# One VectorE addition of p for all four rows, and fixed places for the FFN's VectorE operations

## What is computed

```python
def _derivative(q, p, drive, coupling, bias):
    i_couple = jnp.tanh(q) @ coupling.T
    dq = q - q ** 3 / 3.0 - p + drive + i_couple + bias
    dp = EPSILON * (q + ALPHA - BETA * p)
    return (dq, dp)
# per token: dq1..dq4 at q, q + DT/2 dq1, q + DT/2 dq2, q + DT dq3
q_next = clip(q + DT / 6.0 * (dq1 + 2 * dq2 + 2 * dq3 + dq4), -20, 20)
p_next = clip(p + DT / 6.0 * (dp1 + 2 * dp2 + 2 * dp3 + dp4), -20, 20)
...
h = silu(gate) * up
y = h @ w_down.T
out = x + y / sqrt(mean(y * y) + EPS)
```

## Time and profile before

| | us |
|---|---|
| median of three executions | 1601.17 |
| profiled execution | 1600.72 |
| its span in the trace | 1598.8 |
| VectorE busy | 1521.6 (95%) |
| TensorE busy | 1468.2 (92%) |
| ScalarE busy | 784.6 (49%) |
| GpSimd busy | 48.3 (3%) |

### The profile page before, as it was taken

One profiled execution on the slowest core, in us unless ns is written; L12 is line 12 of the kernel. 1 busy time (PEld: TensorE's weight loads), 2 busy tenths in 40 slices (PEclk: granted clock), 3 DMA queues, 4 the chain that ended last, 5 costly groups with the idle time before them and its releaser, 6 DMA issues.

```text
span 1598.8 us, 97361 instructions
## 1 busy us (share of the span) xinstructions
PE 1468.2 (92%) x39808; PEld 1323.3 (83%) x39808; DVE 1521.6 (95%) x11790; ACT 784.6 (49%) x5087; POOL 48.3 (3%) x49
## 2 busy tenths in 40 slices
PE   0057899999999999999999999999999999999997
PEld 0046788898988898898988989888888989898897
DVE  7989999999999999999999999999999999999992
ACT  4134455555555555545555555555455555555552
POOL 3410000000000000000000000000000000000000
PEclk9999999999999999999999999999999999999999
DMA  9400000000000000000000000000000000000000
GB/s 238 120 6 7 13 7 8 17 8 20 8 7 21 7 21 4 21 7 8 20 8 21 8 17 8 17 11 7 20 8 20 5 20 8 8 21 7 21 4 22
DMA packets 13554, 33.13 MB, mean 21 GB/s; under 512 B 1712, under 2 KB 6064, under 8 KB 12976
## 3 DMA queue, kind: packets, MB, share of 16 engines
q1 hardware_dynamic: 13104, 26.89, 6.4%
HBM read 22.69 MB, written 4.19 MB: 17 GB/s over the span
## 4 chain that ended last, share of the span: by engine, by line
PE 82%; DVE 11%; issue 1%; ACT 0%; POOL 0%; POOLq 0%; DVEq 0%; ACTq 0%
PE scan_ps L584 54%; PE gu_ps L322 19%; PE y_ps L336 9%; DVE q_stage L702 1%; DVE th L663 1%; DVE q_sq L667 1%; DVE q_stage L704 1%; DVE with_q L657 1%; DVE with_p L657 1%; DVE xl L374 1%; DVE scan_ps L675 1%; DVE q_cub L670 1%; DVE p_part L657 1%; DVE q_raw L704 0%; DVE h L353 0%
## 5 line engine op out<-in xcount | busy, mean ns | idle before, releaser
L584 PE MATMUL scan_ps<-th,wscan 128*128 128x32 f16 (+1 forms) x32768 | 1080.3, 175 | 121.6 <-ACT th L620 115.1
L584 PEld LDWEIGHTS scan_ps<-th,wscan 128*128 128x128 f16 x32768 | 956.5, 96 | 255.6 <-ACT th L620 177.1
L620 ACT ACTIVATE th<-q_stage 128x16 f16<-128x16 f32 x1536 | 318.8, 208 | 512.9 <-DVE q_stage L702 512.9
L322 PE MATMUL gu_ps<-xl,wffn 128*128 128x128 f16 x2816 | 384.9, 219 | 0.0
L322 PE MATMUL gu_ps<-xh,wffn 128*128 128x128 f16 x2816 | 384.5, 218 | 0.0
L663 DVE TENSOR_TENSOR th<-t,th 128x16 f16<-128x16 f32 x2048 | 343.6, 168 | 0.0
L622 ACT ACTIVATE t<-q_stage 128x16 f32<-128x16 f32 x1536 | 306.4, 199 | 0.0
L322 PEld LDWEIGHTS gu_ps<-xl,wffn 128*128 128x128 f16 x2816 | 272.8, 97 | 0.3
L322 PEld LDWEIGHTS gu_ps<-xh,wffn 128*128 128x128 f16 x2816 | 262.8, 97 | 0.3
L620 ACT ACTIVATE th<-q_raw 128x16 f16<-128x16 f32 x512 | 106.3, 208 | 206.8 <-DVE q_raw L702 203.3
L428 ACT ACTIVATE sum_r<-dr,constant 128x64 f32<-128x64 f32 x528 | 174.0, 332 | 7.6 <-DMA dr<-drive 7.6
(11 more groups left out here) (43 smaller groups left out, 1018.2 us busy)
## 6 DMA issues: line engine op xcount, KB each, us to landing
raw<-packed SPq DMA_DIRECT2D x11, 768.0 KB, 6.4
dr<-drive SPq DMA_DIRECT2D x34, 128.0 KB, 2.1
sc<-scales SPq DMA_DIRECT2D x11, 384.0 KB, 6.8
xres<-x SPq DMA_DIRECT2D x16, 256.0 KB, 3.5
out<-osb SPq DMA_DIRECT2D x16, 256.0 KB, 2.9
coup<-coupling_t SPq DMA_DIRECT2D x1, 1024.0 KB, 15.0
q_raw<-cond_t SPq DMA_DIRECT2D x1, 16.0 KB, 1.8
bias<-bias_t SPq DMA_DIRECT2D x1, 2.0 KB, 1.7
```

The lines of the kernel that those rows point to most:

```text
L322: i = nc.tensor.matmul(gu_ps[b][:, half * P:(half + 1) * P], wffn[:, u, part, col:col + P], tokens[f.parity][:, kt, :], start=(r == 0), st ...
L584: i = nc.tensor.matmul(to if both else to[:, 0], wscan[:, w, part, kt, cols], moving if both else moving[:, 0], start=first, stop=last, sk ...
L620: nc.scalar.activation(th[s % 2][:, c, 0, :], q[:, c, :], ACT.Tanh, scale=1.0 / S).then_inc(now.tanh_hi, 1)
```

## The change

`UNIT` scales rows 1 to 3 so that p enters every row with the same factor. One addition of 128 columns then forms `with_p` for all four rows, in kind 3, with `p_state` read four times by a broadcast. The row's own unit is multiplied in where the row joins the cube (`local_in` in place of `cube_in`), and the factor of the cube moves into `square`. In kinds 1 and 2 the additions for row 3 and for p that stood between `square` and `low_part` stand behind `local_in`; some move one stage on; the one for q3 moves from the end of kind 2 to the head of kind 3. `Places` gives each h32, hl and norm_out a stage of its own of kind 1 or 2, `hist_low` has stages 1 and 2 with two each, `hh` shares h32's stage, and `DOWN_LAG` is 7.

```diff
-P_ROW = [float(LINEAR[i, BY_P] * P_UNIT) for i in range(ROWS)]
+P_ALL = float(np.float32(LINEAR[0, BY_P] * P_UNIT))
+def row_unit(i):
+    at = np.float32(LINEAR[i, BY_P] * P_UNIT / P_ALL).view(np.int32)
+    near = [float((at + np.int32(k)).view(np.float32)) for k in range(-4, 5)]
+    qs = LINEAR[i, BY_Q1:BY_Q1 + i]
+    return min(near, key=lambda unit: abs(sum(float(np.float32(x / unit)) * unit - x for x in qs)))
+UNIT = [1.0] + [row_unit(i) for i in range(1, ROWS)]
+BY = LINEAR[:-1] / np.array(UNIT)[:, None]
-SHIFT = [(COEF[STAGE_COEF[i]] + LINEAR[i, BY_Q1 + i]) / CUBE[i] for i in range(4)]
+OWN = [COEF[STAGE_COEF[i]] + float(LINEAR[i, BY_Q1 + i]) for i in range(4)]
-LOCALS = STEPS * 23
+LOCALS = STEPS * 20
-DOWN_LAG = 5
+DOWN_LAG = 7
-def off_start(s):
-    return s if s % 4 else s + 1
+class Places:
+    def __init__(self):
+        self.taken = {1, 2}
+    def next(self, s):
+        while s % 4 not in (1, 2) or s % STAGES in self.taken:
+            s += 1
+        self.taken.add(s % STAGES)
+        return s
 class Schedule:
...
+        places = Places()
         self.silu = {s + 1: u for u, s in gate_up.items()}
-        self.h32 = {off_start(s + 2): u for u, s in gate_up.items()}
-        self.hh = {s + 3: u for u, s in gate_up.items()}
-        self.hl = {off_start(s + 4): u for u, s in gate_up.items()}
+        self.h32, self.hh, self.hl = {}, {}, {}
+        for u, s in gate_up.items():
+            at = places.next(s + 2)
+            self.h32[at] = self.hh[at] = u
+            self.hl[places.next(at + 1)] = u
...
-        busy = set(self.h32) | set(self.hl) | {s + STAGES for s in (*self.h32, *self.hl)}
-        free = [s for s in range(self.norm_sum + 3, 2 * STAGES) if s not in busy and s % 4]
-        self.norm_out = {s: n for n, s in enumerate(free[:KT])}
+        self.norm_out = {}
+        for n in range(KT):
+            self.norm_out[places.next(max([self.norm_sum + 3, *self.norm_out]))] = n
...
-        with_p = [sb(f"with_p{i}", [P, KT, B]) for i in range(ROWS)]
+        with_p = sb("with_p", [P, ROWS, KT, B])
...
-                if ffn and s == 0:
-                    act.wait_ge(before.clipped, STEPS)
-                    hist_high(act, now, 0)
-                if ffn and s == 1:
-                    hist_high(act, now, 1)
-                    hist_high(act, now, 2)
-                if ffn and s == 2:
-                    hist_high(act, now, 3)
+                if ffn and s in (0, 1):
+                    if s == 0:
+                        act.wait_ge(before.clipped, STEPS)
+                    for c in range(s * HC, (s + 1) * HC):
+                        hist_high(act, now, c)
...
-            def square(q):
-                return local(nc.vector.tensor_tensor(q_sq[:, :, :], q, q, ALU.mult))
+            def square(i, q):
+                return local(nc.vector.scalar_tensor_tensor(q_sq[:, :, :], q, CUBE[i], q, ALU.mult, ALU.mult))
...
-            def cube_in(s):
+            def local_in(s):
                 i = s % 4
-                nc.vector.scalar_tensor_tensor(local_ps, halves(q_cub[:, :, :]), CUBE[i],
-                                               halves(linear[i][:, :, :]), ALU.mult, ALU.add).then_inc(now.first_half, 1)
-
-            def add_p(row, step):
-                return add(with_p[row][:, :, :], p_state[:, :, :], P_ROW[row], sum_r[:, step % STEPS, row])
+                nc.vector.scalar_tensor_tensor(local_ps, halves(linear[i]), UNIT[i], halves(q_cub[:, :, :]),
+                                               ALU.mult, ALU.add).then_inc(now.first_half, 1)
+
+            def add_p(step):
+                p_rows = p_state[:, :, :].unsqueeze(1).to_broadcast([P, ROWS, KT, B])
+                return add(with_p[:, :], p_rows, P_ALL, sum_r[:, step % STEPS])
+
+            def add_q(to, row, column, q, base):
+                return add(to[:, :, :], q, float(BY[row, column]), base)
...
-                if ffn and s == 1:
-                    hist_low(dve, now, 0)
-                if ffn and s == 2:
-                    hist_low(dve, now, 1)
-                    hist_low(dve, now, 2)
-                if ffn and s == 3:
-                    hist_low(dve, now, 3)
+                if ffn and s in (1, 2):
+                    for c in range((s - 1) * HC, s * HC):
+                        hist_low(dve, now, c)
...
-                if t == HS:
-                    dve.wait_ge(now.sum_r_ready, SUM_R_PARTS)
-                add_p(2, t)
+                if ffn and t == 1:
+                    dve.wait_ge(now.xl_ready, KT)
...
-                ffn_part(s)
-                add_p(3, t)
                 low_part(s, 0)
...
                 s = 4 * t + 1
                 ffn_part(s)
                 dve.wait_ge(now.q_ready, 2 * s)
-                squared = square(q2)
-                add(with_q1[2][:, :, :], q1, float(LINEAR[3, BY_Q1]), with_p[3][:, :, :])
+                squared = square(1, q2)
                 low_part(s, 0)
...
-                cube_in(s)
+                local_in(s)
+                add_q(with_q1[2], 3, BY_Q1, q1, with_p[:, 3])
                 add(p_part[0][:, :, :], p_state[:, :, :], P_SUM[0], q1)
-                add(with_q2[0][:, :, :], q2, float(LINEAR[2, BY_Q2]), with_q1[1][:, :, :])
-                add(with_q2[1][:, :, :], q2, float(LINEAR[3, BY_Q2]), with_q1[2][:, :, :])
+                add_q(with_q2[0], 2, BY_Q2, q2, with_q1[1][:, :, :])
                 finish(s)
 
                 s = 4 * t + 2
                 ffn_part(s)
                 dve.wait_ge(now.q_ready, 2 * s)
-                squared = square(q3)
-                add(p_part[1][:, :, :], p_part[0][:, :, :], P_SUM[1], q2)
+                squared = square(2, q3)
                 low_part(s, 0)
...
-                cube_in(s)
+                local_in(s)
+                p2 = add(p_part[1][:, :, :], p_part[0][:, :, :], P_SUM[1], q2)
+                with_23 = add_q(with_q2[1], 3, BY_Q2, q2, with_q1[2][:, :, :])
+                dve.wait_ge(now.local, p2)
                 add(p_part[2][:, :, :], p_part[1][:, :, :], P_SUM[2], q3)
-                add(with_q3[:, :, :], q3, float(LINEAR[3, BY_Q3]), with_q2[1][:, :, :])
                 finish(s)
 
                 s = 4 * t + 3
-                ffn_part(s)
+                dve.wait_ge(now.local, with_23)
+                add_q(with_q3, 3, BY_Q3, q3, with_q2[1][:, :, :])
                 dve.wait_ge(now.q_ready, 2 * s)
...
                 if t + 1 == HS:
-                    dve.wait_ge(now.sum_r_ready, 2 * KT)
+                    dve.wait_ge(now.sum_r_ready, SUM_R_PARTS)
                 if t + 1 == STEPS:
-                    dve.wait_ge(now.sum_r_ready, SUM_R_PARTS + 2 * KT)
+                    dve.wait_ge(now.sum_r_ready, 2 * SUM_R_PARTS)
                 dve.wait_ge(now.local, p_next)
-                add_p(0, t + 1)
-                add_p(1, t + 1)
+                add_p(t + 1)
                 finish(s)
```

More of the change, by code:

```diff
@@ L429, in sum_drive @@
                                  bias=constant[:, row, c:c + 1],
-                                 scale=float(LINEAR[row, BY_R] * S)).then_inc(done, 1)
+                                 scale=float(BY[row, BY_R] * S)).then_inc(done, 1)
         def sp_store(sp, f, k):
@@ L508, in _ @@
                 for row in range(ROWS):
-                    nc.vector.tensor_scalar(constant[:, row], bias[:, :], float(LINEAR[row, BY_R] * S),
-                                            float(LINEAR[row, BY_ONE] * S), ALU.mult, ALU.add).then_inc(constants, 1)
+                    nc.vector.tensor_scalar(constant[:, row], bias[:, :], float(BY[row, BY_R] * S),
+                                            float(BY[row, BY_ONE] * S), ALU.mult, ALU.add).then_inc(constants, 1)
                 dve.wait_ge(constants, ROWS)
@@ L537, in _ @@
                 dve.wait_ge(sums_set, SUM_R_PARTS)
-                for row in (0, 1):
-                    nc.vector.scalar_tensor_tensor(with_p[row][:, :, :], p_state[:, :, :], P_ROW[row],
-                                                   sum_r[:, 0, row], ALU.mult, ALU.add)
+                p_rows = p_state[:, :, :].unsqueeze(1).to_broadcast([P, ROWS, KT, B])
+                nc.vector.scalar_tensor_tensor(with_p[:, :], p_rows, P_ALL, sum_r[:, 0], ALU.mult, ALU.add)
                 for n, coef in enumerate(COEF):
@@ L644, in dve_block @@
         def dve_block(dve, now, before, ffn, rest):
-            linear = [with_p[0], with_q1[0], with_q2[0], with_q3]
+            linear = [with_p[:, 0], with_q1[0][:, :, :], with_q2[0][:, :, :], with_q3[:, :, :]]
             count = [0]
@@ L714, in dve_block @@
                     dve.wait_ge(before.local, LOCALS)
-                if t == HS:
-                    dve.wait_ge(now.sum_r_ready, SUM_R_PARTS)
-                add_p(2, t)
+                if ffn and t == 1:
+                    dve.wait_ge(now.xl_ready, KT)
                 if t:
-                    if ffn and t == 1:
-                        dve.wait_ge(now.xl_ready, KT)
```

(19 more changed lines are left out.)

3 lines of the change are left out of this document (2 added, 1 removed).

## The result

The changed kernel takes 1562.89 us (median of four executions, 1562.32 to 1563.14) against 1601.2; the ratio is 0.9761, 95% interval 0.9746 to 0.9775. A second series gave 1563.41 us and 0.9762 (0.9749 to 0.9775). The forecast was 1553 with a range of 1536 to 1580: the direction and the range held, but 48 us were forecast and 38 came.

What follows compares the result with a forecast made beforehand. It took the first low part (next reduce 0.73 us later), then VectorE's queue, as the bound. Fifteen blocks save 44.6 us, the first block 2.8, the tail 0.8: 48.2 in all, giving 1553 us, range 1536 to 1580.

Steps and rivals of the forecast that it cites:

- The limit: In each stage the next reduce follows the first low part by 0.73 us; VectorE's queue is a second limit.
- Wide addition: End of kind 3: one 128-column addition costs 0.20 us, the same as the two 32-column ones there.
- Kind 2 with hl: Stages with hl: second reduce 0.17 behind the first, local term at R+0.93, stage 1.38 us.
- The wait for p's sum: In kind 2 the third addition waits for the first: 0.22 us behind it instead of 0.10.
- One sign that the prediction had named for a free wait: Kind 2 no longer than kind 1 would show that VectorE's wait for its own result costs nothing.
- Kind 3: Loses its FFN operation; p's addition stays ahead of the low part at R+0.62: stage 1.35 us.
- The burst stage: One kind 3 stage per block, with the last unit's down matmuls, keeps about 0.77 us extra.
- First block: Earlier low part saves 0.06 us in kinds 1 and 2, 0.04 in kind 0, 0.02 in kind 3: 2.8 us.
- A: Low part does not bind in clean stages; only the FFN stages' 0.07 us goes: 1558 to 1582 us; 30%.
- B: VectorE binds less; all stages fall to 1.33 to 1.345 us, total 1525 to 1536 us; 12%.
- C: The wide addition's broadcast operand is slow in kind 3: 1596 us at 0.41, 1614 at 0.48; 8%.
- D: A down matmul finding hl late stops TensorE's in-order queue, 50 us at 0.3 each: 1603 us; 3%.

Runs made afterwards that it cites:

- W and P without O: The changed kernel with row 3's addition (kind 1) and p's addition (kind 2) back between square and first low part: 1598.01 us, ratio 0.9977.
- W: The kernel before with only the wide addition, rows and FFN operations as before: 1597.51 us, ratio 0.9975.
- the last kernel: The changed kernel with two hist_low as one 256-column operation, the xl wait left out and the cleared-semaphores wait moved: 1558.39 us, ratio 0.9736.

## Why the prediction was right, and where it fell short

- **Where the 10.7 us went.** The profiled execution was to gain 48.2 us and gained 37.5. Of the difference 10.5 us lie in the fifteen blocks. Their mean by kind is 22.10, 22.06, 22.66 and 22.59 us against 21.9, 22.0, 22.4 and 22.4. The first block, the tail and the preparation make up the rest.
- **The limit.** Right: a low part, not TensorE's filling work, sets a stage (W and P without O, fewer matmuls). Wrong in which one: the prediction read 0.73 behind the first low part. The second one binds, 0.53 to 0.54 behind it, and since it mostly lay 0.19 behind the first, the two readings gave the same numbers; that the law held in the sum is in part luck. Where the cube waits for a late square between them, the second one is later than that, and 0.73 is too little.
- **Wide addition.** Right in its price: the reduce stands 0.25 behind it, as it did behind the two narrow ones. Four narrow ones at that place would have given back all but 1 us of the gain.
- **Kind 0** 1.37, kind 1 1.36 and 1.34: as forecast. A pair of hist_low in kind 1 too (1.54 for 1.56).
- **Kind 2 with hl**, the mis-sized term: 1.38 forecast, 1.405 measured. The sum hides two errors that partly cancel. The local term came at R+0.97, not 0.93; behind it stand 0.43 to the next reduce, where the prediction's chain has 0.12 + 0.22 + 0.12 = 0.46 (from 0.93 that gives 1.39, not the 1.38 that it wrote). The step that failed is "the second reduce comes 0.17 behind the first". That holds behind kind 0, where the distance is 0.17. Behind kind 1 it is 0.19 to 0.20, and hl, the square and all that follows stand 0.03 later. Why it is longer there is argued and not tested: kind 1 ends at 1.35 with the low parts' limit at 1.33 to 1.35, so its first reduce is hardly late, and the second has to wait for TensorE's second half. Together 11 stages, two norm_out and the pair, 14 x 0.025 x 15 = 5 us. Empty kind 2 stages, two per block, took 1.34 for 1.37, since there the local term was in time and the chain behind it shorter.
- **The wait for p's sum** in kind 2: 0.22 from addition to addition, as forecast, and of that 0.02 is lost, since another addition fills the rest. Against the rule of the Trainium skill (VectorE: DVE Perf Modes, "The DRAIN you can't avoid") that a semaphore costs nothing extra, a wait on the result right behind does show in these rows, but an operation in between hides nearly all of it. One sign that the prediction had named for a free wait did show in part: empty kind 2 stages take 1.34, no longer than empty kind 1 stages, and they take 1.34 without the addition and its wait as well. There the low parts set the stage and cover the wait. With hl, kind 2 takes 1.40 to 1.41 and kind 1 1.35 to 1.36. The kernel without that addition has no time to show for it, because the next stage gave the gain back.
- **Kind 3** 1.36 for 1.35, and 1.38 behind empty kind 2 stages: 16 x 0.01 x 15 = 2 us. The burst stage went as forecast (0.74 extra for 0.77).
- **Waits by themselves.** The prediction left them out. A second wait ahead of the clip delays it by 0.08 us: stages 4 and 48 take 1.42 (0.05 each), stages 31 and 63, with another wait ahead of the wide addition, 0.03 more, together 0.16 x 15 = 2.4 us.
- **Single late stages** (stage 0 and others, see above) about 2 us, which no row of before announced.
- **The first FFN block** took 90.93 us where the others take 89.3: 1.6 us that the sum did not have. The kernel before had 0.6 of it already (92.28 against 91.64).
- **Tail** 1.2 for 0.8. TensorE's longest waits there, against the earlier trace rows:

```profile
PE y_ps L360 <- DVE hl L389: 1.8, 2, 1.3
```

  1.8 us in place of 2.7: the last unit's wait is shorter by the down matmuls ahead of it.
- **First block** 2.55 for 2.8. Kinds 0 to 2 fell by 0.045 to 0.06 as forecast; kind 3 was to fall by 0.02 and kept its 1.43. Without FFN matmuls the reduce follows the first low part by 0.77 us there, not by 0.73, in the kernel before as well. The prediction set the change of the low part alone into its sum, so this did not hurt.
- **Rivals.** A fell: empty stages of kind 2 go from 1.38 to 1.34, kind 0 from 1.40 to 1.37. B fell: the queue binds in kind 0, where VectorE's last addition starts 0.13 ahead of the reduce and the stage takes 1.37. Its range was also reckoned wrong: blocks of 86.5 to 87.5 us (64 x 1.345 with the same extras is 87.5, not 87.2) would give 1520 to 1535, not 1525 to 1536. C fell with the wide addition's 0.29. D fell: TensorE's waits for hl in the whole scan sum to under 1 us.

## What to carry to other kernels

In a loop that passes from engine to engine, mark where each queue releases the next engine; an operation ahead of that mark costs its full issue time, one behind it costs nothing until the queue itself is full. An edit that is worth nothing alone can be worth 23 of 38 us together with the others, so take a change apart with its parts combined and not one by one only. When two signals move together in every row, the rows can't say which one binds; move one of them before building on either. And before you give a small gain to an edit, compare the same stage over all repetitions: here single late stages made up about half of what W seemed to lack and half of what the last kernel gained.

## What the runs showed of the hardware

- Independent VectorE operations of 32 columns start 0.10 us apart at a duration of 0.18; 128 columns hold the queue 0.20 (h32 to square, 792.66 to 792.86), 256 columns 0.33, four times 32 about 0.41.
- An operation that waits for the one right before it on VectorE starts 0.22 behind it; a second wait ahead of the clip adds 0.08.
- A GpSimd addition of 0.25 us beside a VectorE operation with two SBUF operands stretched that from 0.19 to 0.26 us.
- A stage that ends late because of VectorE gives part of that back: its two reduces lie 0.15 to 0.17 apart, not 0.20 (0.12 behind the four narrow additions). Removing such lateness therefore brings less than it seems, in one kernel nothing.
- In the changed kernel all eleven single late stages of blocks 3 to 15 have an 8 KB transfer of instructions on queue 14 that begins 0.9 to 1.8 us behind their first reduce; that the one causes the other is not shown.
